# Two fused adapter + expert layers: the main product over two token chunks in seven block products instead of eight

## The reference

```python
# cond: dense product, bias, and one low-rank adapter (rank 16) chosen per sample
y = x @ W0.T + b0 + scale[id] * (x @ A[id].T) @ B[id].T
# ffn: dense product, bias, and 8 experts of rank 16, two of which each token takes
w  = renormalised top-2 of softmax(y @ Wr.T)              # (tokens, 8)
out = y @ W1.T + b1 + 2 * (w-weighted (y @ LA)) @ LB      # 1024 outputs
```

## Time and profile before

| | |
|---|---|
| Runs (us) | 753.58, 755.16, 753.55; median 753.58 |
| Profiled execution | span 753.2 us from first to last instruction; the runs' median is 0.4 us above it |
| PE busy | 740.6 us, 98% of the span, 3524 matmuls |
| DVE / ACT / POOL busy | 290.7 / 136.2 / 120.1 us |
| Transfers | 60.83 MB, mean 81 GB/s |
| Granted TensorE clock | 0.999 of full over the span |

### The profile page before, as it was taken

How to read it: one execution, slowest core, us unless ns; L and a number is a source line. 1 busy time by engine, 2 the same in 40 slices (tenths; PEclk the granted TensorE clock), 3 DMA queues, 4 the chain that set the end, 5 groups by cost and what they waited for, 6 DMA issues and landing times.

```text
span 753.2 us, 9733 instructions
## 1 busy us (share of the span) xinstructions
PE 740.6 (98%) x3524; PEld 635.9 (84%) x3524; DVE 290.7 (39%) x539; ACT 136.2 (18%) x223; POOL 120.1 (16%) x118
## 2 busy tenths in 40 slices
PE   5999999999999999999999999999999999999998
PEld 5999998888788788788889999978878887887886
DVE  5355356305402611630545444652163054035211
ACT  5221214101200300212032121240021022003000
POOL 0510001104102300410206000030041041023002
PEclk9999999999999999999999999999999999999999
DMA  8220114203301500450253110260052043023002
GB/s 310 74 71 28 56 56 138 91 0 126 122 0 70 174 3 0 156 171 0 84 200 105 35 56 28 62 196 24 19 162 65 0 136 110 0 84 107 0 14 97
DMA packets 30117, 60.83 MB, mean 81 GB/s; under 512 B 5652, under 2 KB 8084, under 8 KB 30102
## 3 DMA queue, kind: packets, MB, share of 16 engines
q1 hardware_dynamic: 28566, 58.56, 23.4%
q0 software_dynamic: 1536, 2.10, 1.0%
HBM read 41.47 MB, written 19.16 MB: 80 GB/s over the span
## 4 chain that ended last, share of the span: by engine, by line
PE 97%; DMA 2%; DVE 1%; SPq 0%; ACT 0%; issue 0%
PE ps L290 30%; PE ps L291 30%; PE ps L292 29%; PE ps L358 4%; PE ps L391 2%; DMA e_raw<-in_ext 2%; PE ps L375 1%; PE ps L346 1%; PE ps L402 0%; DVE e_hl L534 0%; ACT e_hl L423 0%; PE ps L369 0%; DVE out_st L727 0%; SPq L183 0%; SPq L190 0%
## 5 line engine op out<-in xcount | busy, mean ns | idle before, releaser
L290 PE MATMUL ps<-x_hl,p_hl 128*128 128x512 f32 x576 | 228.7, 397 | 0.0
L291 PE MATMUL ps<-x_hl,p_hl 128*128 128x512 f32 x576 | 227.6, 395 | 0.0
L292 PE MATMUL ps<-x_hl,p_hl 128*128 128x512 f32 x576 | 226.7, 394 | 0.0
L773 POOL TENSOR_TENSOR out_st<-x_hl 128x512 f32<-128x512 f32 x64 | 91.7, 1460 | 562.9 <-DMA out_T<-out_st 196.3
L290 PE MATMUL ps<-e_hl,w_hl 128*128 128x388 f32 (+1 forms) x432 | 148.4, 343 | 9.0 <-DVE e_hl L534 9.0
L292 PE MATMUL ps<-e_hl,w_hl 128*128 128x388 f32 (+1 forms) x432 | 147.5, 342 | 0.0
L291 PE MATMUL ps<-e_hl,w_hl 128*128 128x388 f32 (+1 forms) x432 | 147.5, 341 | 0.0
L290 PEld LDWEIGHTS ps<-x_hl,p_hl 128*128 128x128 f32 x576 | 108.1, 188 | 25.8
L292 PEld LDWEIGHTS ps<-x_hl,p_hl 128*128 128x128 f32 x576 | 108.2, 188 | 25.6
L291 PEld LDWEIGHTS ps<-x_hl,p_hl 128*128 128x128 f32 x576 | 108.4, 188 | 24.4
L727 DVE TENSOR_TENSOR out_st<-ps,out_st 128x512 f32<-128x512 f32 x64 | 43.7, 690 | 158.1 <-PE ps L292 145.9
(11 more groups left out here) (74 smaller groups left out, 406.3 us busy)
## 6 DMA issues: line engine op xcount, KB each, us to landing
x_st<-in_xT SPq DMA_DIRECT2D x32, 256.0 KB, 3.8
x_scratch<-out_st SPq DMA_DIRECT2D x32, 256.0 KB, 2.4
x_st<-x_scratch SPq DMA_DIRECT2D x32, 256.0 KB, 3.5
out_T<-out_st SPq DMA_DIRECT2D x32, 256.0 KB, 2.4
e_raw<-in_ext SPq DMA_DIRECT2D x14, 580.0 KB, 8.5
w_raw<-in_w SPq DMA_DIRECT2D x14, 512.0 KB, 3.4
stack<-bw_scratch SPq DMA_DIRECT2D x24, 144.0 KB, 2.6
bw_scratch<-bw_st SPq DMA_DIRECT2D x4, 388.0 KB, 3.1
```

What stands on the lines that cost most here:

```text
L290: nc.tensor.matmul(dst, w_hi, m_hi, start=start, stop=False)
L291: nc.tensor.matmul(dst, w_hi, m_lo, start=False, stop=False)
L292: return nc.tensor.matmul(dst, w_lo, m_hi, start=False, stop=stop)
L773: nc.gpsimd.tensor_tensor(out_st[:, m % SLOTS, :], x_hl[:, m, 0, :].bitcast(f32), x_hl[:, m, 1, :].bitcast(f32), ALU.add).then_inc(S["resi ...
```

## The change

The 1024 x 1024 product of a chunk pair is written as a 2 x 2 block product (halves of the outputs and of the features; and two chunks of 512 tokens, 0 and 1, side by side) and done with seven block products M1 to M7 of sums of blocks in place of eight. With A the folded weight and B the tokens: M2 = (A21+A22) B11, M4 = A22 (B21-B11), M5 = (A11+A12) B22, M3 = A11 (B12-B22), M1 = (A11+A22)(B11+B22), M7 = (A12-A22)(B21+B22), M6 = (A21-A11)(B11+B12). A pair of chunks (a "super", `g`) is PE's new unit: four supers in all, two a layer.

- **Fold.** ACT copies each row tile to `p_raw`, POOL makes the five weight sums of a pair of row tiles (`form_sums`), ACT and DVE split all seven forms (`form_split`), and SP stores them to DRAM (`store_forms`). `p_hl` is gone; only the expert and router columns stay (`px_hl`). The forms come back through a ring of seven slots, one slot for each output tile of a block product (`load_ring`, 28 per super, 4 KB a partition).
- **Tokens.** Both chunks of a super are held whole (`x_raw`). POOL makes the five token sums (`x_sums`, 20 tiles per super); they are split like x. The residual is now x itself.
- **Outputs.** ACT and DVE keep M2, M5 and combinations in `s2`, `s4`, `s5`, POOL does 16 further adds per super, and each output tile is stored from there.
- **Program.** PE's, ACT's, DVE's, POOL's and SP's loops over chunks and rows are written out; the k order of the fold is plain; `stack`, `low_mv` and `rlog` have a buffer for each chunk of the pair.

The diff, cut to its core. SP:

```diff
+            def store_forms(l, pair):
+                for i, j in enumerate(SPLITS):            # SPLITS = (M4, M2, M3, M5, M1, M7, M6)
+                    sp.wait_ge(S["form_lo"], NM * (KH * l + pair) + i + 1)
+                    sp.dma_start(forms[l, j, :, :, pair, :], f_hl[:, j, ...]).then_inc(d_form[j], 16)
+            def load_ring(l, g, n):
+                j, m = n // KH, n % KH
+                sp.wait_ge(d_form[j], 16 * KH * (l + 1))
...
+                if n >= NM or g % SUPER:
+                    sp.wait_ge(S["pe_m"], 28 * g + n - NM + 1)
...
+                load_x(l, 0, 0, range(KT))
+                store_forms(l, KH - 1)
                 sp.wait_ge(S["w0_lo"], RT * (l + 1))
...
                 sp.dma_start(lb_raw[:, 1, :], lb[l]).then_inc(S["d_lb"], 16)
+                for n in range(NM):
+                    load_ring(l, SUPER * l, n)
+                load_x(l, 0, 1, range(KT))
                 for ob, (o, n) in enumerate(OB):
+                    sp.wait_ge(S["bw_lo"], NOB * l + ob + 1)
+                    sp.dma_start(bw_dram[l, :, :, o:o + n], bw_st[:, :, o:o + n].bitcast(f32)).then_inc(S["d_bw"], 16)
...
                 sp.wait_ge(S["d_bw"], 64 * (l + 1))
+                load_stack(l, 0, 0)
+                load_stack(l, 0, 1)
```

PE, one super (between the two parts shown stand M4, four output tiles, the second chunk's routers and M5; after them M1, M7, output tiles, M6, output tiles):

```diff
+            def product(g, j, m, bank, start):
+                n = 4 * j + m
+                pe.wait_ge(d_ring[n % NM], 16 * (4 * g + n // NM + 1))
+                for k in range(KH):
+                    last = split_product(ps[:, bank, :], a_hl[:, n % NM, k, 0, :], a_hl[:, n % NM, k, 1, :],
+                                         x_hl[:, slot, k, 0, :], x_hl[:, slot, k, 1, :], ...)
...
+                    routers(l, g, 0)                      # the 16 and the 24 matmuls
...
+                    product(g, M2, 0, BANK_C21[0], True)
+                    logits(l, g, 0)                       # waits low_lo and d_stack
+                    for m in range(1, KH):
+                        product(g, M2, m, BANK_C21[m], True)
+                    transposes(g, 0)
+                    pe.wait_ge(S["x_lo"], NT * g + T_D1 + KH)
...
+                        product(g, M3, m, BANK_C12[m], False)
+                    pe.wait_ge(S["hg_lo"], 2 * g + 2)
+                    for m in range(KH):
+                        pe.wait_ge(S["e_done"], KH * g + m + 1)
+                        low_and_experts(0, 1, m, BANK_C12[m])
```

DVE and POOL:

```diff
+                dve.wait_ge(S["d_bw"], 64 * (l + 1))
+                dve.wait_ge(S["d_bias_rows"], 96 * (l + 1))
...
+                    gated(g, 1)
+                    for m in range(2):
+                        keep_e(g, m)
+                    sum_split(g, M6, T_E3, range(2))
+                    keep_e(g, 2)
+                    sum_split(g, M6, T_E3, range(2, 4))
+                    keep_e(g, 3)
...
+                    pool.wait_ge(S["pe_hx"], 2 * g + 2)
+                    x_sums(g, M3, (1, 0), (1, 1), ALU.subtract)
+                    for m in range(KH):
+                        pool.wait_ge(S["s5_done"], KH * g + m + 1)
...
+                        nc.gpsimd.tensor_tensor(s4[:, m, :], s4[:, m, :], s5[:, m, :], ALU.subtract)
+                        nc.gpsimd.tensor_tensor(s2[:, m, :], s2[:, m, :], s5[:, m, :], ALU.add)
...
+                        nc.gpsimd.tensor_tensor(s4[:, m, :], s4[:, m, :], x_raw[:, 0, m, :], ALU.add)
+                    pool.wait_ge(S["pe_m"], 28 * g + 4 * (M5 + 1))
+                    x_sums(g, M6, (0, 0), (1, 0), ALU.add)
```

More of the change, by code:

```diff
@@ new lines, in fused_layers @@
+        s4 = place("s4", [P, KH, CH], f32)
+        s5 = place("s5", [P, KH, CH], f32)
+        p_raw = place("p_raw", [P, 2, 2, EXT], f32, keep_at)
+        bw_st = place("bw_st", [P, 2, EXT], f32r, keep_at)
+        acc = place("acc", [P, EXT], f32, keep_at + 4 * EXT * 4)
+        assert 5 * EXT * 4 <= at[0] - keep_at
+        px_hl = place("px_hl", [P, KT, 2, HX], f32r)
+        stack = [place(f"stack{i}", [STACK, D + ER], f32r) for i in range(2)]
+        lb_at = at[0]
+        lb_hl = place("lb_hl", [P, 2, D], f32r)
@@ L129, in fused_layers @@
         mul_sb = place("mul_sb", [2 * LOW, BATCH], f32)
[L130 removed]
+        rlog = [place(f"rlog{i}", [SROWS, NE], f32) for i in range(2)]
         bwr = place("bwr", [P, NE], f32)
@@ L187, in load_first @@
[L187 to L201, removed]
+                    g = SUPER * l - 1
@@ L229, in load_stack, with load_row @@
-            def load_stack(l, c):
-                for i, hl in enumerate((0, 1, 0)):
[L232 to L237, removed]
+            def load_row(l, r):
+                sp.wait_ge(S["pe_unit"], UNITS * l + (r - 1) * NOB)
+                sp.dma_start(w0_raw[:, r % 2, 1, :], w0[l, k_of(r)]).then_inc(d_w0[r % 2], 16)
@@ new lines, in logits @@
+            def logits(l, g, tb):
+                u = 2 * g + tb
+                pe.wait_ge(S["low_lo"], u + 1)
+                pe.wait_ge(d_stack[tb], 64 * (g + 1))
+                pe.wait_ge(S["d_bias_rows"], 96 * (l + 1))
+                nc.tensor.matmul(ps[:, H_BANK, :], stack[tb][:, D:D + ER], low_mv[tb][:], start=False,
+                                 stop=True).then_inc(S["pe_h"], 1)
+                pe.wait_ge(S["sxr_done"], u + 1)
+                for t in range(TT):
+                    last = nc.tensor.matmul(ps[:, S_BANK, t * NE:(t + 1) * NE], sx[:, t * P:(t + 1) * P],
+                                            rlog[tb][:], start=True, stop=True)
+                last.then_inc(S["pe_logit"], 1)
@@ new lines, in sum_split, with chain @@
+            def sum_split(g, j, place, ks):
+                slot = SLOT_OF[j]
+                for k in ks:
+                    dve.wait_ge(S["x_hi"], NT * g + place + k + 1)
+                    sub(x_hl[:, slot, k, 1, :], x_sum[:, slot, k, 1, :],
+                        x_hl[:, slot, k, 0, :].bitcast(f32)).then_inc(S["x_lo"], 1)
+            count = [0]
+            def chain(ins, wait=True):
+                ins.then_inc(S["dve_step"], 1)
+                count[0] += 1
+                if wait:
+                    dve.wait_ge(S["dve_step"], count[0])
@@ L734, in chunk @@
                     elif l + 1 < LAYERS:
                         first(l + 1)
-                    finish(range(6, KT))
-                with dve.Fori(0, NCH - 1) as c:
-                    chunk(c, False)
-                chunk(NCH - 1, True)
+                    for m in range(KH):
+                        out_c11(g, m)
+                    if more:
+                        x_split(g + 1, 0, 1)
+                    for m in range(KH):
+                        out_c22(g, m)
+                    if not more and l + 1 < LAYERS:
+                        rest(l + 1)
```

1123 lines of the change are left out of this document (701 added, 422 removed).

## The result

The changed kernel takes 805.75 us (median of 4 runs, 804.73 to 807.63), against 753.57 for the kernel before on the same chip: 1.0687 times as long, interval 1.067 to 1.0704. The forecast was 767.6 in 748 to 788: the direction holds, the size does not.

A forecast was written before the change was run, and what follows sets the result against it. It took PE's matmul count and pace as the bound. 753.2 - 44.7 - 0.9 + 46.0 + 11.6 + 2 = 767.2 us of span, with the median 0.4 above: 767.6 us, range 748 to 788.

The forecast's parts named there:

- What goes: PE's main matmuls: 336 in place of 384 per super, 192 fewer at 0.2327 us each, -44.7 us.
- The boundary's 0.9: PE's wait at the layer boundary, on the very last output, would go: -0.9 us.
- The layer's start: PE waits before the logits for the queued adapter row, landing near 43: 20.2 plus 2.8 a layer, +46.0 us.
- The table's sum: Transfers queued at a layer's start up to the adapter row's end: 13.25 MB in 38.2 us, piece by piece.
- dense queue: Rival, 12%: layer-start transfers all run at 432 GB/s, landing at 35.5, 31.0 us in all, 752.6 us.
- stores that overtake: Rival, 8%: adapter row's stores don't wait behind earlier transfers; landing at 31, +8 + 2.8 a layer, 743 us.
- The gates' hand-offs: Tight hand-offs at the gates (D2, M3's token sum), taken with the fold as +2 in all, bounds 0 and 12.
- The rival that named the mechanism: Rival, 14%: GpSimd and DVE shut each other out, splits wait a whole add; +5 a super, 788 us.
- The wait in each super: Between M3 and its outputs, PE waits for `keep_e` behind M6's splits: +2.9 a super, +11.6 us.
- Fold: Form stores delay a later even row's load: 0 to 3 us at two places a layer, within the +2.
- Half rate: After the long wait at each layer's start PE runs at the lower clock, losing 2.8 us a layer.
- Ring and unrolling: Ring loads never hold PE and unrolling's extra instruction fetch costs 0; rival that ring can't keep up: 3%, 843 us.

The follow-up runs named there:

- c_no_adds: Changed kernel with POOL's 12 output adds per super left out, so outputs lack those terms: 758.24 us.
- a_bw_first: Changed kernel with SP's order alone altered: adapter row stored behind two ring loads, not seven and x of chunk 1: 791.13 us.
- b_gates_first: Changed kernel with POOL's order alone altered: its 12 output adds wait until both chunks' gates are made: 795.77 us.
- i_best: h_waits with the fold's even row of W0 loaded behind two of a pair's seven form stores, not all: 728.56 us, 0.967 of the kernel before.
- h_waits: Changed kernel with a_bw_first's and b_gates_first's orders, keeps and outputs before M6's splits, and DVE's and ACT's adapter/bias-row waits moved later: 736.89 us.
- p_back: Kernel before plus 12 junk POOL adds per chunk beside routing, without pause, one broadcast column as both inputs: routing chain 10.8 us, launch 753.72.
- p_two: Kernel before plus 12 junk two-input POOL adds per chunk beside routing, a semaphore between each: routing chain 7.61 us, launch 755.52.
- j_best: i_best with the adapter row stored behind four of the last pair's seven form stores and one ring load: 733.53 us, 0.9741 of the kernel before.
- p_one: Kernel before plus 12 junk one-input POOL copies per chunk beside routing: routing chain 5.17 us, launch 753.83.
- p_zero: Kernel before plus 24 junk POOL memsets per chunk beside routing, no input: routing chain 3.95 us, launch 754.45.

## Why the prediction was right or wrong

- **What goes: right.** 3332 matmuls. c_no_adds bears out the size: its span of 756.5 less the added waits (36.9 + 4.5 + 3.3) is 711.8, 3.3 above 708.5. Two things that partly cancel are in these 3.3: about 9 us of added half rate, and some 6 us of a faster pace (0.227 for 0.232 us a matmul), which the sum, with 0.2327 for all, didn't have. The boundary's 0.9 is gone as forecast: `e_hl` was waited for three times, 9.0 us, and now twice, 8.4, both at the launch's start.
- **The layer's start: right, with luck in the pieces.** Landing at +43 as worked out; waits of 37.4 against 40.4. The table's sum holds (about 38.7 us for 38.2), its rows don't: by the packets' sizes in the trace x of chunk 0 took 6.8 us (7.7 forecast), the stores in 1 KB pieces 11.6 (9.9; 342 GB/s in the stretch above, not 371), the 4 KB rows 11.3 (9.7), x of chunk 1 5.4 (7.7; 384 GB/s, not 274) and the adapter row some 3.6 (3.2). The errors cancel. a_bw_first shows that the order is the cause. The rivals of the dense queue (landing at 35.5) and of stores that overtake are out, though single stretches did run at 419.
- **The gates' hand-offs: wrong, and this is the step that failed.** The prediction wrote "with the gates' tight hand-offs ... I take +2 in all", with the fold in it. It gave the second chunk's routing, which DVE does while POOL makes its 12 adds, no price of its own; a +2 leaves it near the 3.65 us of the kernel before. It is 12.85. The term came out as 27.6 (gates) + 8.9 (`x_hl`) of waits and 12.9 beside them, nearly all half rate, 49.4 in all; its bound was 12. Less the 11.6 of the wait that didn't appear, the 49.4 are 37.8, and the miss is 38.2; the other terms are each off by a few us and happen to cancel, the faster pace among them.
- **The rival that named the mechanism was undersized.** It put +5 a super on the 0.69 us splits, which a full wait makes 1.96. But a full wait is paid by each operation, not by each column: ten operations of the routing are held, by 0.45 to 1.14 us each and 9.2 in all, and PE's wait of 6.9 leaves 2.3 that the chain had to spare. The argument against it, a split of 1.35, was a misreading: 5.39 / 4 is the mean of four merged splits, and the last of them ran alone. The second and the third by themselves, and POOL's adds beside them, in the kernel before:

```profile
246.78 1.67 DVE L534 TENSOR_TENSOR x_hl<-x_st,x_hl 128x512 fp32r<-128x512 f32 x1
248.37 1.78 DVE L534 TENSOR_TENSOR x_hl<-x_st,x_hl 128x512 fp32r<-128x512 f32 x1
```

```profile
246.24 1.66 POOL L773 TENSOR_TENSOR out_st<-x_hl 128x512 f32<-128x512 f32 x1
247.86 1.74 POOL L773 TENSOR_TENSOR out_st<-x_hl 128x512 f32<-128x512 f32 x1
```

  The first three (the first took 1.38) each end 0.55 us after an add ends, so each had to let the running add finish, and 0.69 alone became up to 1.78. The hold until an add's end, on which the +38 us rest, was there to be read in the trace of before.
- **The wait in each super: right in place, hidden by the other.** It isn't in the changed kernel, and it is in b_gates_first, with 6.5 a super for the 2.9; how long it would be with the adds in their old place and the gates on time, no run shows.
- **Fold: the size was nearly right, the cause half.** 5.2 us in all, one wait of it 4.0, above the "up to 3 us" of a place. The transfer is late as said (the even row's load is issued after 8 us of form stores; i_best, with the load earlier, has no such wait, and its median is 8.3 below h_waits' run). But DVE is held up ahead of it too: the subtraction of the row before takes 7.20 for the 1.22 that it takes alone, through all five of POOL's sums, and the forms' splits, and with them the stores, come after it. In i_best that subtraction still takes 6.67, and PE doesn't wait.

```profile
41.86 7.20 DVE L764 TENSOR_TENSOR w_hl<-w_raw,w_hl 128x1024 fp32r<-128x1024 f32 x1 [3.52 <-ACT w_hl L562]
```

- **Half rate: right in kind, counted at too few places.** 2.8 for each long wait was counted at two places, and there it is 3.2 and 2.9; each of the four supers has one more (3.2 in c_no_adds' account) and the fold one of about 1.6. That is some 20 against 5.6; the faster pace hides 6 of it.
- **Ring and unrolling: right.** The ring's 3.2 us are at its first use in a layer alone, and no wait for instructions shows.

What stays open: by how much the held subtraction counts in the fold apart from the late load wasn't tried alone; and p_back differs from p_two in its inputs too, so the pause between adds is the likeliest reason for 7.61 against 10.8, not the only one left.

## What to carry to other kernels

Work handed to POOL "because POOL is idle" is priced by the number of DVE operations that run beside it, not by their size: in the changed kernel ten operations, nine of them on 4 to 32 columns, lost 9 us. Keep POOL's two-input adds out of the stretch in which DVE runs a chain of short operations, each needing the one before, that another engine waits for; here one wait on POOL does it, and with the other reorderings of i_best the change goes from 7% slower to 3% faster. And where transfers queue, place the small store that others wait for ahead of the large loads that have time; but look at how the waits are cut up and not only at their sum: in the first layer j_best's three waits of 8.6 us in all cost 6.6 us of half rate, i_best's two of 8.9 only 2.8.

## What the runs showed of the hardware

- Adds on POOL back to back hold nearly each tensor-tensor and tensor-scalar operation of DVE for one add; with a semaphore between the adds about every second one passes at once (p_two, 7.61 for 10.8 us). Copies hold about every second one, mostly for 0.3 to 0.4 us (p_one), memsets the tensor-scalar ones alone, for 0.15 (p_zero).
- A DVE operation can miss several turns: 7.20 us for 1.22, through five adds in a row, though in rows 9 and 10 each split got in behind the add that was running.
- Short waits can be followed by the lower clock too: in j_best one of 2.0 us, by a stretch at 0.57. The 1.4 us for the ring in i_best was not: the clock stayed at 1.00 until 144, 5 us later. Behind the gates' wait of 6.89 the four transposes take 1.12 us for 0.44, and PE is at the lower level for 8 us.
- SP took 1.19 us for each 512 KB store in 1 KB pieces (8.31 / 7), and 0.75 for each ring load (5.25 / 7).
